# Two 16-head attentions: six split products, position rows placed by DMA from small tiles, slopes made on POOL beside the norm, first load issued before the second batch's splits

## The reference, cut to what matters

```
# L3_attn_b: each query block of 128 sees its own and both neighbour blocks
scores = einsum('bhnqd,bhnkd->bhnqk', qb, k_ctx) / sqrt(8)
win_ok = abs(rel) <= 128
weights = softmax(where(win_ok & valid, scores, -inf)); out = weights @ v_ctx @ Wo.T + bo
# L1_attn_a: slopes = 2 ** (-0.5 * h), h = 1..16
bias = -slopes[:, None, None] * where(causal, dist, 0.0)   # dist = |query - key|
attn = softmax(where(causal, q @ k.T * 8 ** -0.5 + bias, -inf)); out = attn @ v @ Wo.T
```

## Time and profile before

| | us |
|---|---|
| three executions, median | 3575.45 |
| lowest, highest | 3564.14, 3583.17 |
| the profiled execution, its own time | 3585.18 |
| its span, from first to last instruction | 3583.1 |
| L1 attention in it (1195 to about 1550) | about 355 |
| L3 attention in it (3189 to about 3468) | about 280 |

### The profile page before, as it was taken

How to read it: one execution, slowest core, us unless ns; L and a number is a source line. 1 busy time by engine, 2 the same in 40 slices (tenths; PEclk the granted TensorE clock), 3 DMA queues, 4 the chain that set the end, 5 groups by cost and what they waited for, 6 DMA issues and landing times. The chain is left out here.

```text
span 3583.1 us, 54951 instructions
## 1 busy us (share of the span) xinstructions
PE 2880.5 (80%) x21418; PEld 1480.1 (41%) x21486; DVE 1859.3 (52%) x3533; ACT 1405.9 (39%) x2681; POOL 765.2 (21%) x632
## 2 busy tenths in 40 slices
PE   6565878778888498989768888998888877768986
PEld 3454247423357234434322222342332434555555
DVE  5311245478964388711378888203763543536733
ACT  3211424432234246642356777422221222234652
POOL 1000006245617201000443340003530001230003
PEclk9666869878889789989879999997998989878987
DMA  2022001121101422100031010000510001023302
GB/s 109 15 63 74 0 12 45 37 72 65 53 20 51 112 44 37 21 1 0 14 70 28 12 24 1 0 0 17 145 49 0 0 1 48 20 71 62 51 6 70
DMA packets 86479, 136.40 MB, mean 38 GB/s; under 512 B 13319, under 2 KB 52199, under 8 KB 84947
## 3 DMA queue, kind: packets, MB, share of 16 engines
q1 hardware_dynamic: 79187, 118.50, 13.1%
q0 software_dynamic: 7040, 14.43, 1.5%
HBM read 106.81 MB, written 25.85 MB: 37 GB/s over the span
## 5 line engine op out<-in xcount | busy, mean ns | idle before, releaser
L1655 ACT ACTIVATE at_pt<-PS 128x384 f32<-128x384 f32 (+3 forms) x704 | 288.5, 455 | 237.7 <-PE PS L1567 202.5
L1705 DVE TENSOR_REDUCE at_mp<-PS 128x1 f32<-128x384 f32 (+3 forms) x640 | 313.5, 538 | 115.1 <-PE PS L1555 98.9
L1552 PE MATMUL PS<-at_kx,at_qx 72*128 72x384 bf16 (+5 forms) x640 | 219.0, 347 | 66.8 <-DMA at_kx<-L_attn_a_parts 26.8
L1565 PE MATMUL PS<-at_qx,at_kx 105*128 105x512 bf16 (+5 forms) x704 | 214.4, 314 | 7.8 <-ACT at_pt L1655 5.9
L4300 DVE CUSTOM_DVE_ANT_0 PS<-PS,ls_pt 128x1024 f32<-128x1024 f32 x128 | 153.8, 1237 | 19.1 <-ACT ls_pt L4153 15.5
L4153 ACT ACTIVATE ls_pt<-PS,ls_far 128x512 f32<-128x512 f32 x256 | 155.5, 686 | 18.6 <-PE PS L3974 10.1
L2425 DVE TENSOR_TENSOR_SCAN mb_ring<-PS,mb_ring 128x1024 f32<-128x1024 f32 x64 | 146.6, 2291 | 19.4 <-POOL mb_ring L2364 6.7
L2380 PE MATMUL PS<-mb_ring,ident 128*128 128x512 f32 x256 | 147.2, 728 | 6.0 <-DVE mb_ring L2430 6.0
L1227 DVE SCALAR_TENSOR_TENSOR X<-PS,small_L,X 128x512 f32<-128x512 f32 x8 | 6.0, 751 | 261.2 <-PE PS L1175 261.2
L2409 ACT ACTIVATE PS<-mb_dt,mb_a 128x1024 f32<-128x1024 f32 x64 | 71.5, 1118 | 174.8 <-DVE mb_ring L2425 169.5
L1578 PE MATMUL PS<-at_pt,at_v 128*9 128x256 f32 (+3 forms) x1408 | 130.7, 451 | 5.5 <-issue 1.4
(11 more groups left out here) (825 smaller groups left out, 6557.2 us busy)
## 6 DMA issues: line engine op xcount, KB each, us to landing
rw_arena<-rw_v_rows SPq DMA_DIRECT2D x32, 512.0 KB, 4.6
dl_arena<-in_fir_bank SPq DMA_DIRECT2D x32, 256.0 KB, 3.1
lnA<-mb_rows SPq DMA_DIRECT2D x16, 512.0 KB, 3.7
XN<-mb_rows SPq DMA_DIRECT2D x16, 512.0 KB, 3.7
ffn_place<-in_ffn_L SPq DMA_DIRECT2D x4, 1152.0 KB, 16.7
at_qx<-L_attn_a_parts SPq DMA_DIRECT2D x24, 192.0 KB
at_kx<-L_attn_a_parts SPq DMA_DIRECT2D x72, 64.0 KB
at_qx<-L_attn_b_parts SPq DMA_DIRECT2D x24, 192.0 KB
```

Of the source, the lines that this page charges most:

```text
L1552: mm = nc.tensor.matmul(PS[:, n % 3, 0:e - c], QX[0:RAW, u % 3, g, blk(i, P)], KX[0:RAW, u % 3, g, c:e], start=True, stop=True)
L1565: mm = nc.tensor.matmul(PS[:, 3 + n % 3, 0:e - c], KX[0:FULL, u % 3, g, blk(j, P)], QX[0:FULL, u % 3, g, c:e], start=True, stop=True)
L1655: nc.scalar.activation(PT[:, y % SLOTS, g, 0:e - c], PS[:, 3 + n % 3, 0:e - c], ACT.Exp, scale=SCALE).then_inc(exp_done, 1)
L1705: nc.vector.tensor_reduce(best, sc, AX.X, ALU.max).then_inc(s_maxed, 1)
```

## The change

The three lowest of the nine products (middle by low, low by middle, low by low) are no longer formed: the contraction is over 48 rows of data. `QX` is loaded by 6 DMAs of 8 rows, `KX` by 3 of 24, 16 and 8 rows. For L1 the slope rows (48 to 53) come by 4 more DMAs in each load, one for each head, from `SLT`, which is now a tile of 6 rows by 16 heads by 128 columns, each read 8 times. `load` thus issues 13 DMAs for L1 (12 before, 13 for u < 3) and 9 for L3 (12 before). POOL writes no slope rows in the projection and attention stages; the waits for `rows_ready` are gone. The slopes are cut by POOL in the norm stage, with masks made from the identity; the wide fills of `QX` and `KX` are replaced by one fill of `UNIT` (128 by 1024, ones). `row_kinds`, `position_rows` and ACT's `KROWS` are gone. The position rows are placed straight from `PHI`, `PLO` and `UNIT`, 3 rows of each to all 12 places (3 slots, 4 heads), for L3 from `UNIT` alone, and these DMAs are issued after the stores of m = 0. `load(sp, 0)` is issued after the stores of m = 3, ahead of those of m = 4. Masks are issued by functions of their own in the same order as before (`LANES` is 1). The contraction is over 54 and 57 rows for L1, 48 and 51 for L3.

```diff
-    MROW = 102 if causal else 72
-    RAW, FULL = (102, 105) if causal else (72, 75)
+    LANES, SPLIT = 1, ((0, 0), (0, 1), (0, 2), (1, 0), (1, 1), (2, 0))
+    SLOPES = 6 if causal else 0
+    PLACE = 8 * len(SPLIT)
+    RAW = PLACE + SLOPES
+    FULL = RAW + 3
...
+                for p, (c, _) in enumerate(SPLIT):
+                    sp.dma_start(QX[top + 8 * p:top + 8 * p + 8, u % 3, :, :], parts[0, heads, c, :, tokens].rearrange("g d t -> d g t")).then_inc(LOADED[u % 3], 16)
+                for at, n in ((0, 3), (24, 2), (40, 1)):
+                    sp.dma_start(KX[top + at:top + at + 8 * n, u % 3, :, :], parts[1, heads, 0:n, :, tokens].rearrange("g c d t -> (c d) g t")).then_inc(LOADED[u % 3], 16)
+                if causal:
+                    for g in range(EACH):
+                        slopes = SLT[0:SLOPES, heads.start + g, :].unsqueeze(1).to_broadcast([SLOPES, 8, SEQ // 8])
+                        sp.dma_start(QX[top + PLACE:top + RAW, u % 3, g, :].rearrange("p (r t) -> p r t", r=8), slopes).then_inc(LOADED[u % 3], 16)
...
-                    own(pool.memset(QX[64:96, :, :, :], 0.0))
-                else:
-                    own(pool.memset(KX[64:96, :, :, :], 1.0))
+                    for n in range(3):
+                        own(pool.tensor_tensor(RM[:, n:n + 1], k.ident[:, n:n + 1], k.ident[:, n + 3:n + 4], ALU.add))
+                    own(pool.tensor_copy(SH[:, 0, :], SL[:, :]))
...
+                    own(pool.tensor_copy(SLT[0:SLOPES, :, :], SLR[0:SLOPES, 0, :].unsqueeze(2).to_broadcast([SLOPES, 16, SEQ // 8])))
+                own(pool.memset(UNIT[:, :], 1.0))
...
-                        if m == 4:
+                        if m == 0:
+                            for lane in range(LANES):
+                                for n, rows in enumerate(KROWS):
+                                    at = 64 * lane + PLACE + 3 * n
+                                    sp.dma_start(KX[at:at + 3, :, :, :].rearrange("p s g t -> p (s g) t"), rows[0:3, :].unsqueeze(1).to_broadcast([3, 3 * EACH, SEQ])).then_inc(PLACED, 16)
+                        if m == 3:
                             for n in range(4):
                                 sp.wait_ge(STORED[n], 48)
-                            if causal:
-                                sp.wait_ge(rows_made, 1)
-                                for slot in range(3):
-                                    sp.dma_start(KX[96:105, slot, :, :], KROWS[96:105, :].unsqueeze(1).to_broadcast([9, HG, SEQ])).then_inc(PLACED, 16)
                             load(sp, 0)
...
-                        pool.tensor_copy(QX[96:102, u % 3, :, :], SLT[96:102, HG * r:HG * r + HG].unsqueeze(2).to_broadcast([6, HG, SEQ])).then_inc(rows_ready, 1)
```

More of the change, by code:

```diff
@@ L1359, in load @@
         def load(sp, u):
[L1360 to L1368, removed]
+            tokens = blk(u // 4, SEQ)
+            for lane in range(LANES):
+                heads = slice(HG * (u % 4) + EACH * lane, HG * (u % 4) + EACH * lane + EACH)
+                top = 64 * lane
+                for p, (c, _) in enumerate(SPLIT):
[6 more added lines that the diff above has]
+                        sp.dma_start(QX[top + PLACE:top + RAW, u % 3, g, :].rearrange("p (r t) -> p r t", r=8), slopes).then_inc(LOADED[u % 3], 16)
         with ExitStack() as early:
@@ L1550, in score @@
                     if n >= 3:
                         pe.wait_ge(s_maxed, n - 2)
-                    mm = nc.tensor.matmul(PS[:, n % 3, 0:e - c], QX[0:RAW, u % 3, g, blk(i, P)], KX[0:RAW, u % 3, g, c:e], start=True, stop=True)
-                    for j in range(c // P, e // P):
-                        if j == i if causal else j != i:
-                            mm = nc.tensor.matmul(PS[:, n % 3, j * P - c:(j + 1) * P - c], k.identb[:, :], ABOVE[:, 0 if j >= i else 1, :], start=False, stop=True, skip_group_check=True)
@@ L1556, in score, with score_masks @@
-                    mm.then_inc(s_ready, 1)
-                def score_turned(u, x, g):
-                    n = N2 * u + HG * x + g
+                    rows = lane_rows(lane, RAW)
+                    mm = nc.tensor.matmul(PS[:, n % 3, 0:e - c], QX[rows, u % 3, g, blk(i, P)], KX[rows, u % 3, g, c:e], start=True, stop=True)
+                    if not masks_first(x):
+                        mm.then_inc(s_ready, 1)
+                def score_masks(u, x, t):
+                    n = N1 * u + HG * x + t
+                    i, c, e = first[x]
+                    for j in masks_first(x):
+                        mm = nc.tensor.matmul(PS[:, n % 3, j * P - c:(j + 1) * P - c], k.identb[:, :], ABOVE[:, 0 if j >= i else 1, :], start=False, stop=True, skip_group_check=True)
+                    if masks_first(x):
+                        mm.then_inc(s_ready, 1)
@@ L1560, in score_turned @@
+                def score_turned(u, x, t):
+                    n = N2 * u + HG * x + t
                     h, j, c, e = second[x]
-                    if x == opens[h] and g == 0:
-                        pe.wait_ge(LOWERED[h], 16 * (u + 1))
+                    lane, g = divmod(head_second(t), EACH)
+                    if x == opens[h] and t == 0:
+                        pe.wait_ge(LOWERED[h], 16 * LANES * (u + 1))
                     if n >= 3:
                         pe.wait_ge(exp_done, n - 2)
-                    mm = nc.tensor.matmul(PS[:, 3 + n % 3, 0:e - c], KX[0:FULL, u % 3, g, blk(j, P)], QX[0:FULL, u % 3, g, c:e], start=True, stop=True)
+                    rows = lane_rows(lane, FULL)
+                    mm = nc.tensor.matmul(PS[:, 3 + n % 3, 0:e - c], KX[rows, u % 3, g, blk(j, P)], QX[rows, u % 3, g, c:e], start=True, stop=True)
+                    if not cuts[x]:
+                        mm.then_inc(st_ready, 1)
```

106 lines of the change are left out of this document (44 added, 62 removed).

## The result

The changed kernel takes 4017.27 us (median of 4, 4011.28 to 4036.51) against 3574.15 us for the kernel before in the same comparison (median of 4): a ratio of 1.1241, 95% interval [1.1208, 1.1274]. It is 12% slower; the forecast was 0.7% faster. The profiled execution took 4013.72 us.

A forecast was written before the change was run, and what follows sets the result against it. PE was taken to order the work, though not fed without gaps, with SP's queue bounding the projection stages. Gains of 16.0 + 6.2 + 4.6 = 26.8 us off the 3575.45 us median gave 3548.7 us, range 3536 to 3561.

The forecast's parts named there:

- Products left out cost PE no time: Score matmuls of both attentions: fewer contraction rows change nothing for PE, since the number of matmuls is the same; 0 us.
- Rival 3: Both attentions: scores on fewer rows let the granted clock fall to 1.2 GHz; 3664 at half of L1's stage; chance 0.04.
- The prediction's own sign of failure: Steady attention stages: the prediction fails if, among other signs, their clock is under 0.95.
- POOL's slope copies: L1's attention stage: five copies that slow a DVE pad go, 3.3 us a period; gain 16.0 us, bounds 13 to 19.
- Norm stages: Shorter POOL fills let the next stage start sooner: 3.4 us in L1, 2.1 us in L3.
- L1's projection stage: SP's queue sets the first score at +37.0 from the stage's start; gain 6.2 us, the norm stage's 3.4 included.
- The stores were held for 4 us: L1's projection stage: three placing copies of 3 rows delay the stores behind them, taken as 4 us between 0 and 5.5.
- the upper end of its reckoning: L1's placing copies: 3 rows use three DMA engines, 9.8 us in all, delaying the stores by 5.5 us.
- L3's projection stage: SP's queue sets the first score at +28.5; gain 4.6 us, 2.1 of it the norm stage's; copy delay 0.4 us.
- The moved load as what the starts are worth: L3's projection stage: the 4.6 us gain, 2.1 the norm's, is what it is worth; stores then hold the barrier.
- The sum of 26.8 us: Whole kernel: 16.0 for the slope copies, 6.2 for L1's start and 4.6 for L3's; ratio 0.9925.

The follow-up runs named there:

- e1: Kernel before, only score matmuls cut to 54 and 57 rows in L1, 48 and 51 in L3: 4076.39 us against 3618.76 on the same chip.
- e4: Changed kernel plus 24 rows of zeros in `QX` and `KX`, so scores use 78, 81, 72 and 75 rows: 3592.12 us, ratio 0.9941 to the kernel before.
- e6: e4 with POOL's seven copies of 6 x 4096 put back at the old moments, into rows nothing reads: 3610.80 us, ratio 0.9981.
- e5: e4 with the placing copies issued by SP in the norm stage instead of after the stores of m = 0: 3583.99 us, ratio 0.9906.
- e7: e4 with the first load moved back behind the stores of m = 4: 3591.51 us, ratio 0.9928.
- e11: Changed kernel with only PE's order changed, one head at a time: score, turned score, then masks of both: 3679.66 us.
- e13: Changed kernel with mask matmuls also on 64 rows and mask tiles of zeros, so nothing is masked: 3670.65 us.
- e10: e4 with fewer rows of zeros, 7 in L1 and 17 in L3 (scores of 61, 64, 65 and 68 rows): 3750.66 us.

## Why the prediction was wrong

The step that failed is "Products left out cost PE no time: 102 rows and 72 rows take 329 and 328 ns for the same 384 columns". Both counts in the earlier trace rows are above 64, and both were read as durations. The changed kernel's 54 and 48 rows fall on the other side of a step, and the cost lies between the starts of neighbours of different kinds, where no row of a single shape can show it. It is 0.11 us for each change; the 2240 changes of both attentions come to some 245 of the 449 us (an estimate, since part of them falls on waits). The other 200 us or so go with the granted clock, which fell to 0.67 and 0.52. That the changed row count does both is shown (e1, e4); which share of the fall of the clock is due to the changes and which to the few rows is open.

Rival 3 named the clock and the row count and the right place, with a chance of 0.04. What spoke against it had the same gap: L3 at 72 rows was granted as much as L1 at 102, and both lie above 64. Its price of 3664 took half of L1 alone at the lower level; both attentions were hit, L3 nearly whole, and the changes themselves come on top. The prediction's own sign of failure, a clock of the steady stages under 0.95, came true.

The other steps, measured where the changes are absent (e4 and its kin):

- POOL's slope copies, forecast 16.0 us: 15.2 (e6 less e4; L1's scores in e4 are 13.4 us shorter than before). All pads at 0.19 us, as said. Right.
- Norm stages, forecast 3.4 and 2.1 us: 3.6 and 2.1. Right.
- L1's projection stage, forecast 2.8 us of its own (first score at +37.0): +38.9, a gain of 0.9. The stores were held for 4 us, as taken; 3 rows do run on three engines (e5), the upper end of its reckoning; mis-sized were the third copy's issue (2.5 us, not 0.8) and the 13 loads (7.1 us from 1223.95 to 1231.04, not 6.1). The first load came at +23.1, forecast +22.3.
- L3's projection stage, forecast +28.5: +29.7. One copy of 3 rows delayed the nine stores by 2.0 us, not 0.4; e5 gives 3.0 us back there.
- The moved load as what the starts are worth: it is worth nothing or less (e7), so the starts' gain comes from the rest: 3.6 and 2.1 us of it is the norm stage, and how the rest divides between the position rows and the smaller load was not measured.
- The sum of 26.8 us: e4, the change without its changes of row group, gains 16.9 us in L1 and 2.9 in L3 by its stages, 19.8 in all; of the shortfall 1.9 us is its own zeros in L1's start. Its ratio was 0.9941 where 0.9925 was forecast.

## What to carry to other kernels

Before a contraction is shortened, look at what stands beside it in PE's order: a matmul of at most 64 rows next to one of 128 pays at each change. Filling the rows to 65 or more with zeros took the loss away (e4); putting narrow matmuls next to narrow ones, or making both narrow, took most of it away but left a lower clock (e11, e13). Compare starts, not durations, over one repeat of the pattern, and set them against the columns; busy time and single durations hide this. A DMA of few rows can hold up the stores behind it (one of 3 rows delayed nine stores by 2 us, three by 4); issue it where SP has nothing urgent behind it, as in e5.

## What the runs showed of the hardware

- The change between at most 64 and more rows costs 0.11 us at either clock level. With 1151 and 1089 of them a stage was granted 0.52 and 0.67, where it had 1.00 and 0.98 without, and PE was recorded busy for 99% and 98%. The Trainium skill, "TensorE: Matmul & The Clock Gate", Part 1, has the clock follow how busy PE is. Here the changed kernel is recorded busier in L3 (99% against 92%) at the lower clock, and the measurement decides: the recorded busy share doesn't tell the clock.
- In e10, 17 rows of zeros took far longer to copy than 24 in e4. The windows in which only these copies ran, e4 and then e10 (the last two columns are the share of the DMA engines and GB/s):

```profile
3198.00:3200.00 2.00, 2.00 (x6) 0.95 (x5) 0.69 (x1) 1.97 (x4) 0.21 (x1) 1.00 0.75 147
```

```profile
3350.00:3360.00 10.00, 5.74 (x13) 2.11 (x12) 2.77 (x4) 6.59 (x11) 1.52 (x3) 0.95 0.06 24
```

24 rows ran on 0.75 of 16 engines, that is 12, at 147 GB/s; 17 rows on 0.06, one engine, at 24 GB/s, and the stores behind them came late, which is L3's longer start in e10. The rule of "DMA: Bandwidth & Descriptors" in the Trainium skill, How many engines, gives 12 and 1 for these counts; the trace agrees.
- The same copy of `UNIT` took 2.51 us to issue as the third of its kind in L1 and 0.83 us as the only one in L3. Waiting for the copies ahead would explain it; no run tests that.
